# Softmax sums as a by-product of ScalarE's exponentials, and the mixing, x's rounding and two rounds of weight sums at other quarters

## The reference, cut to what matters

```python
W = weights[condition]                       # (32, 64, 64)
xm = jnp.einsum('bct,bcd->bdt', x, W)        # the mixing
q, k, v = xm @ Wq.T, xm @ Wk.T, xm @ Wv.T    # q and k normalised by head
scores = jnp.einsum("bkgqd,bksd->bkgqs", qg, k) / math.sqrt(HD)
attn = jax.nn.softmax(scores + bias[None], axis=-1)
x = x + (attn @ v) @ Wo.T
x = x + ffn(low_rank(x))
```

## Time and profile before

| | |
|---|---|
| median of 3 runs | 2375.29 us (2374.58 to 2379.8) |
| the profiled execution | 2375.95 us, span 2374.0 us |
| granted TensorE clock, mean | 0.997 |
| TensorE busy | 2344.8 us, 99% of the span |
| VectorE busy | 1776.3 us, 75% |
| ScalarE busy | 1464.5 us, 62% |
| GpSimd busy | 285.1 us, 12% |

### The profile page before, as it was taken

One profiled execution on the slowest core, in us unless ns is written; L12 is line 12 of the kernel. 1 busy time (PEld: TensorE's weight loads), 2 busy tenths in 40 slices (PEclk: granted clock), 3 DMA queues, 4 the chain that ended last, 5 costly groups with the idle time before them and its releaser, 6 DMA issues.

```text
span 2374.0 us, 33429 instructions
## 1 busy us (share of the span) xinstructions
PE 2344.8 (99%) x11706; PEld 1961.6 (83%) x11706; DVE 1776.3 (75%) x2930; ACT 1464.5 (62%) x3625; POOL 285.1 (12%) x336
## 2 busy tenths in 40 slices
PE   8999999999999999999999999999999999999998
PEld 6877888888888888888888888888888888888886
DVE  6777969696847878787846777777876696969691
ACT  4246767576625857576824857576844676767660
POOL 1222010101011001010021101010021101010111
PEclk9999999999999999999999999999999999999999
DMA  6774434442542242423443242423244242423250
GB/s 254 265 262 187 160 134 155 147 135 73 195 150 89 86 145 74 148 72 134 143 153 116 72 160 71 160 72 124 97 172 144 81 150 70 151 80 139 73 197 36
DMA packets 88440, 316.16 MB, mean 133 GB/s; under 512 B 12716, under 2 KB 13228, under 8 KB 87124
## 3 DMA queue, kind: packets, MB, share of 16 engines
q1 hardware_dynamic: 70292, 247.14, 30.1%
q0 software_dynamic: 16256, 62.92, 7.2%
q10 hardware_dynamic: 1728, 3.98, 0.5%
HBM read 282.54 MB, written 31.46 MB: 132 GB/s over the span
## 4 chain that ended last, share of the span: by engine, by line
PE 94%; DVE 3%; DMA 1%; issue 1%; ACT 0%; POOL 0%; ACTq 0%; POOLq 0%; DVEq 0%
PE main L1041 80%; PE qt_bank L1202 3%; PE s_bank L1218 3%; PE s_bank L1219 2%; PE pv_bank L1239 1%; PE pv_bank L1238 1%; PE pt_bank L1226 1%; PE pt_bank L1041 1%; DVE ring L1511 1%; DVE setup L1511 0%; PE qt_bank L1139 0%; PE s_bank L1139 0%; DMA acc<-in_x 0%; DMA t_scratch<-sums 0%; DMA mask<-in_masks 0%
## 5 line engine op out<-in xcount | busy, mean ns | idle before, releaser
L1041 PE MATMUL main<-ring,act_hi 128*128 128x512 f32 x3584 | 1148.4, 402 | 0.4 <-DVE ring L1511 0.3
L1041 PEld LDWEIGHTS main<-ring,act_hi 128*128 128x128 f32 x3584 | 641.5, 189 | 114.3 <-issue 3.1
L1041 PE MATMUL main<-ring,act_lo 128*128 128x512 f32 x1792 | 701.7, 392 | 0.0
L1041 PE MATMUL main<-ring,lefts 128*128 128x512 f32 x2688 | 625.9, 391 | 0.0
L1041 PEld LDWEIGHTS main<-ring,lefts 128*128 128x128 f32 x2688 | 499.9, 188 | 101.5
L1511 DVE TENSOR_TENSOR ring<-raw,ring 128x1024 fp32r<-128x1024 f32 x448 | 550.5, 1233 | 41.1 <-ACT ring L1249 38.9
L1249 ACT ACTIVATE ring<-raw 128x1024 fp32r<-128x1024 f32 x448 | 472.0, 1056 | 172.0 <-PE main L1041 149.6
L1041 PEld LDWEIGHTS main<-ring,act_lo 128*128 128x128 f32 x1792 | 336.9, 188 | 74.9
L1850 POOL TENSOR_TENSOR rstd<-mean,half 128x4 f32<-128x4 f32 (+1 forms) x192 | 174.0, 906 | 1535.1 <-DVE mean L1636 1535.0
L1382 ACT ACTIVATE sq<-main 128x128 f32<-128x128 f32 x640 | 169.3, 277 | 76.1 <-PE main L1041 72.2
L1410 ACT ACTIVATE prob<-score,peak 128x64 f32<-128x64 f32 x512 | 136.1, 336 | 98.1 <-DVE peak L1694 97.4
(11 more groups left out here) (168 smaller groups left out, 2554.3 us busy)
## 6 DMA issues: line engine op xcount, KB each, us to landing
raw<-in_wq SPq DMA_DIRECT2D x128, 512.0 KB, 4.3
raw<-t_scratch SPq DMA_DIRECT2D x128, 512.0 KB, 3.2
raw<-in_wo SPq DMA_DIRECT2D x96, 512.0 KB, 3.2
raw<-in_wkv SPq DMA_DIRECT2D x64, 512.0 KB, 3.9
sums<-in_wo POOLq DMA_DIRECT2D x32, 512.0 KB, 7.6
t_scratch<-sums POOLq DMA_DIRECT2D x32, 512.0 KB, 4.1
raw<-f_scratch SPq DMA_DIRECT2D x32, 512.0 KB, 4.9
acc<-in_x POOLq DMA_DIRECT2D x16, 512.0 KB, 4.1
```

Source lines behind the costliest of these rows:

```text
L1041: mm = eng.matmul(bank, a, b, start=start and n == 0 and m == 0, stop=stop and n == len(terms) - 1 and m == 2, skip_group_check=further)
```

## The change

Three edits.

1. The exponentials write the sum of each row as well (`accum_out=total`), and the stage `total` on VectorE is gone: `inverse` waits for `exp` in its place. Each of the 512 exponentials becomes two instructions on ScalarE, the second an ACTIVATION_READ_ACCUMULATOR.
2. At the seams of blocks `mix_split` goes from 7.4 to 8.4 and `mix` from 9.8 to 10.5, and the keys' transposes and their parts from (2.8, 3.4, 3.9) to (3.8, 4.35, 4.38) in the `mixing` row.
3. Two of the five rounds of weight sums begin two quarters later, at 20.5 and 37 in place of 18.5 and 35.

```diff
-          mix_split=7.4, mix=9.8, reload=5.1,
+          mix_split=8.4, mix=10.5, reload=5.1,
...
-KEYS_AT = dict(mixing=(2.8, 3.4, 3.9), queries=(3.8, 4.4, 4.9), projection=(4.8, 5.4, 5.9))
+KEYS_AT = dict(mixing=(3.8, 4.35, 4.38), queries=(3.8, 4.4, 4.9), projection=(4.8, 5.4, 5.9))
...
-ROUND_AT = (0.5, 18.5, 35, 104, 180)
+ROUND_AT = (0.5, 20.5, 37, 104, 180)
...
-            for stage in ("total", "inverse", "prob"):
+            for stage in ("inverse", "prob"):
...
-                        act = eng.activation(prob[:, cols], score[:, cols], ACT.Exp, bias=peak[:, r:r + 1], scale=-1.0)
+                        act = eng.activation(prob[:, cols], score[:, cols], ACT.Exp, bias=peak[:, r:r + 1], scale=-1.0,
+                                             accum_out=total[:, r:r + 1])
...
-                elif stage == "total":
+                elif stage == "inverse":
                     k, = key
                     w.wait_ge("exp", k)
-                    eng.tensor_reduce(total[:, :], prob[:, :].rearrange("p (r n) -> p r n", n=SEQ), AXIS.X,
-                                      ALU.add).then_inc(done[stage], 1)
-                elif stage == "inverse":
-                    k, = key
-                    w.wait_ge("total", k)
                     eng.reciprocal(inv[:, :], total[:, :]).then_inc(done[stage], 1)
```

## The result

The changed kernel takes 2386.86 us (median of 5 runs, 2385.69 to 2388.59), the kernel before 2376.64 (5 runs, 2374.58 to 2379.8): a ratio of 1.0043 with a 95% interval of 1.0029 to 1.0057. Forecast were slower and 2385.6, with a range from 2378.5 to 2391. The span of the profiled execution grew from 2374.0 to 2383.6, by 9.6.

A forecast was written before the change was run, and what follows sets the result against it. TensorE, busy 2344.8 of 2374.0 us, was taken as the bound, so only its waits count. Terms 9.8 - 1.5 + 2.0 = +10.3 gave 2386.2 for the profiled execution, 2385.6 as forecast median; range 2378.5 to 2391.

The forecast's parts named there:

- The seams, +9.8: Three block seams: mixing one quarter later makes TensorE wait four times each, 11.3 us less 1.4 lost there today.
- The chain of 4.42: One tile's mixing at a seam: from its start to the matmul needing the last act_lo, 4.42 us, unshortened.
- The keys, 0: Keys' transposes at the seams move along one quarter with the mixing; no waits of note, so 0 us.
- The softmax, -1.5: Softmax sums moved from VectorE to ScalarE: a third of 4.5 us of TensorE's qn waits goes, -1.5 us.
- the late x: Second seam: x landing late costs 0.81 us today; the later rounding and mixing were to cover it.
- the stall: First block, before 180.04: TensorE's 4.11 us wait for qn, hanging on loads before an rstd; predicted to stay.
- The rounds, +2.0: Block 0: two rounds' sums two quarters later lengthen the qn waits at 206.29 and 238.42, together +2.0 us.
- The sum: Whole kernel: 9.8 - 1.5 + 2.0 = +10.3 us, forecast 2385.6 us.
- The clock did not fall at the seams: Rival: four close waits per seam lower TensorE's clock, three times 3.4 us more, 2395.8 us; 7%.
- Relief for VectorE: Rival: relief takes all 4.5 us of qn waits and mixing costs only +7; +2.5, 2377.8 us; 13%.
- ScalarE did not become the late engine: Rival: longer exponentials push ScalarE's weight copies, 0.05 us wait in 128 steps, +6.4, 2392 us; 4%.
- One sign of being wrong: Signs named: seam waits under 0.3 us, the clock falling there, or the loaded stretches growing.

The follow-up runs named there:

- e2: Only mix_split 8.4 and mix 10.5 on the kernel before, keys, rounds and total as they were; 2385.20 us, ratio 1.0036.
- e9: The changed kernel with four VectorE operations per tile's mixing instead of eight, lower-part product left out (less exact); 2373.95 us, ratio 0.9988 to before.
- e3: Only the keys' transposes and parts moved to (3.8, 4.35, 4.38) on the kernel before; 2380.79 us, ratio 1.0017.
- e6: The changed kernel with the keys' transposes and parts put back to (2.8, 3.4, 3.9); 2384.18 us, ratio 1.0026 to the kernel before.
- e13: The changed kernel with the keys' upper part at 4.1 instead of 4.35, ahead of the next step's squares on ScalarE; 2386.32 us, ratio 1.0036 to before.
- e1: Only the softmax sums written by ScalarE's exponentials on the kernel before, all three tables as before; 2369.88 us, ratio 0.9975.
- e12: e10 with the first moved round's loads at 22 but its sums earlier, from 26.8, and the second round back at 35; 2364.66 us, ratio 0.9947 to before.
- e11: e10 with mix_split at 8.4, x's rounding a quarter later, mix still at 9.8; 2376.35 us, ratio 0.9999 to before.
- e4: Only the two rounds of sums moved to 20.5 and 37 on the kernel before; 2380.27 us, ratio 1.0016.
- e10: e1 with the two rounds at 22 and 38.5, so the first round's loads stand behind one more rstd; 2370.05 us, ratio 0.9966 to before.

## Why the forecast held, point by point

- *The seams, +9.8.* Measured: four waits of 0.57, 1.19, 1.05 and 1.05 against 0.50, 1.18, 1.04 and 1.04; three seams cost 11.6, less some 1.6 before: +10.0. The chain of 4.42 is in the rows to a hundredth. e2 and e9 show the cause.
- *The keys, 0.* Wrong: **+3.0**. I looked at where the keys' transposes stand and not at where their two parts went in ScalarE's and VectorE's lists (the step "the keys' transposes move along one quarter with the mixing, and key and value steps have no waits of note"). An engine's list is in order: what matters is not only who needs the moved piece, but what stands behind it. e3, e6 and e13 show it.
- *The softmax, -1.5.* The mechanism was right, the term too small: the starts of the transposes give 5.0 in the loaded stretches, in e1 and in the changed kernel alike. Two rougher ways agree: e1's span is 6.9 less than before, of which about 1 is the late x and 1.7 the clock behind the stall (0.86 from 174 to 186 in e1, 0.72 before), which leaves 4.2; and what is left over of the changed kernel's span is 5.3 (10.0 + 3.0 + 1.9 - 5.3 = 9.6). So **-4 to -5.5**. The step that failed is the bound: I had taken it, 4.5 us, from the rows of waits for `qn` and then a third of it, and these rows leave out waits that show under other names (`issue` in front of the scores, `prob`), or nowhere.
- *The rounds, +2.0.* Measured +1.9. The stall stayed. In place of two waits for `qn` of 0.79 idle stand two of 1.92 (at 239.42 the row reads `[1.92 <-DVE qn L1657]`); the wait of 0.5 behind the stall and that of 0.8 in front of the scores at 232 are gone, and the one in front of the scores at 201 grew from 0.12 to 0.73.
- *The sum.* +10.3 forecast, +9.6 in the span: two errors of +3.0 and some -3.5 cancel. That the total is right to a microsecond is luck; the working is right in two of its four terms.
- *Rivals.* The clock did not fall at the seams: 1.00 in all rows of seams with four waits of up to 1.2. Relief for VectorE did reach the small waits, more than the rival said, and the mixing cost its full price. ScalarE did not become the late engine. One sign of being wrong did come: 0.84 us idle in a loaded stretch (730 to 1250), which is the keys' wait. The addition is better on ScalarE here: 0.38 us on an engine with idle time for 0.42 on the one that TensorE waits for. The Trainium skill ("ScalarE: Activation LUTs", "Rules for kernel authors") has additions on VectorE rather than on ScalarE, as faster there for each element (its figure is for bf16, the sums here are fp32). For sums that the exponentials write out as they go the measurement says otherwise: e1's ratio is 0.9975.

## What to carry to other kernels

A piece of work that is moved brings its own serial chain with it: compare the length of that chain with the busy engine's work left between it and its user, and do it for each piece that shares the table entry, on every engine's list. When the busiest engine's waits are shorter than its overlap, busy time does not show them; compare the starts of the same instructions in both traces instead, or count instructions in equal stretches for a rough figure. And where one number places both a load and the work that uses it, look whether they are bound by different neighbours: here taking them apart (e1 to e12, 0.9975 to 0.9947) gave as much as the best of the three edits.

## What the runs showed that I had not expected

A wait of 2.1 us lowers TensorE's clock in some executions and not in others. The same wait, in the changed kernel (first fence: the stretch holds it) and in e6 (second and third):

```profile
200.00:210.00 10.00, 7.51 (x42) 6.30 (x42) 9.04 (x15) 6.72 (x23) 4.86 (x8) 1.00 0.97 345
```

```profile
206.00:212.00 6.00, 5.44 (x23) 4.44 (x23) 3.86 (x8) 4.37 (x16) 1.79 (x4) 0.72 0.96 362
240.00:246.00 6.00, 5.31 (x21) 4.30 (x22) 3.82 (x8) 4.35 (x14) 0.76 (x2) 0.72 0.98 340
```

```profile
206.56 0.66 PE L1202 MATMUL qt_bank<-ident,qn 128*128 128x128 f32 x4 [1.92 <-DVE qn L1657]
```

In the profiled executions here there are 14 waits of 2.05 to 2.12 us. After six of them the lower clock follows (e6 and e13 both, e3 and e11 one each), at 1.7 us a time (0.28 x 6 in e6), after eight it doesn't (the changed kernel and e9 both, e4 three, e10 one). After the waits of up to 1.5 us it never does; after two of 3.2 it does once (e10) and once not (e11); after the stall it always does, but for a mean of 0.72 in some executions and 0.86 in others. It may be part of the spread between runs of one kernel, which no run here shows, and it makes e6's profiled span some 3.4 too long for a comparison term by term.
